# A decoder layer on one core: the work of all five engines put in another order

## The reference

```python
x = _layernorm(x + _L0_attn_ref(x, W_qkv, W_out))                 # 16 heads of 16, segments of 128, every second key
x = _layernorm(x + _L0_xattn_ref(x, ctx_1024, ctx_1024, Wq, ...)) # 77 context rows
x = _layernorm(x + _L0_ffn_ref(x, router_w, w1, b1, w2, b2))

# _L0_ffn_ref
logits = x @ router_w                         # 14 experts
assignments = jnp.argmax(logits, axis=-1)
weights = jnp.take_along_axis(jax.nn.softmax(logits, axis=-1), assignments[:, None], axis=1)[:, 0]
hid = jax.nn.gelu(jnp.einsum('nd,edf->nef', x, w1) + b1, approximate=False)
all_out = jnp.einsum('nef,efd->ned', hid, w2) + b2
moe_out = jnp.take_along_axis(all_out, assignments[:, None, None], axis=1)[:, 0, :] * weights[:, None]
```

## Time and profile before

| | |
|---|---|
| median of 3 runs | 597.56 us (596.89 to 598.15) |
| the profiled execution | 593.98 us, of it 592.2 us span |
| mean granted clock of TensorE | 0.977 of full speed |
| PE busy | 560.5 us, 95% of the span |
| DVE busy | 463.3 us, 78% |
| POOL busy | 405.7 us, 69% |
| ACT busy | 343.1 us, 58% |
| chain that ended last | PE 74%, POOL 9%, issue 7%, DVE 5% |

### The profile page before, as it was taken

One profiled execution on the slowest core, in us unless ns is written; L12 is line 12 of the kernel. 1 busy time (PEld: TensorE's weight loads), 2 busy tenths in 40 slices (PEclk: granted clock), 3 DMA queues, 4 the chain that ended last, 5 costly groups with the idle time before them and its releaser, 6 DMA issues.

```text
span 592.2 us, 16640 instructions
## 1 busy us (share of the span) xinstructions
PE 560.5 (95%) x5608; PEld 474.9 (80%) x5608; DVE 463.3 (78%) x1071; ACT 343.1 (58%) x842; POOL 405.7 (69%) x554
## 2 busy tenths in 40 slices
PE   7989999999999999999999999799799999999990
PEld 5867788788888888788788778568789999999990
DVE  3778999999999999999999989865455555666661
ACT  2456666666666676676666765546545555555540
POOL 4446675678678677678678766675787677777652
PEclk9899999999999999999999999969989999999996
DMA  7416026126225314313514101114343333333200
GB/s 216 162 24 191 14 52 196 27 68 183 42 60 160 65 40 137 103 51 88 153 34 144 52 10 37 34 39 119 53 112 97 85 87 87 95 92 89 68 16 0
DMA packets 76692, 50.11 MB, mean 85 GB/s; under 512 B 39222, under 2 KB 70970, under 8 KB 76608
## 3 DMA queue, kind: packets, MB, share of 16 engines
q1 hardware_dynamic: 71264, 40.60, 25.5%
q0 software_dynamic: 5344, 8.44, 5.5%
HBM read 40.55 MB, written 10.60 MB: 86 GB/s over the span
## 4 chain that ended last, share of the span: by engine, by line
PE 74%; POOL 9%; issue 7%; DVE 5%; ACT 2%; DMA 1%; POOLq 0%; ACTq 0%; DVEq 0%
PE ps_r L822 15%; PE ps_r L740 13%; PE ps_s L956 11%; PE ps_r L972 10%; PE ps_r L807 5%; PE ps_r L902 5%; PE ps_s L762 4%; PE ps_s L753 3%; POOL token_lists L1579 3%; POOL prob L1498 2%; PE ps_r L795 2%; PE ps_r L879 2%; PE ps_r L897 2%; PE ps_r L904 2%; POOL out L1605 1%
## 5 line engine op out<-in xcount | busy, mean ns | idle before, releaser
L1498 POOL TENSOR_TENSOR prob<-prob,rden 128x616 f32<-128x616 f32 (+1 forms) x96 | 138.4, 1449 | 56.8 <-DVE rden L1173 55.1
L999 ACT COPY probT<-ps_r 128x512 f32<-128x512 f32 x192 | 86.8, 480 | 43.2 <-PE ps_r L740 41.4
L1141 DVE TENSOR_REDUCE mx<-ps_s 128x8 f32<-128x616 f32 (+1 forms) x96 | 88.8, 925 | 19.1 <-PE ps_s L753 12.8
L1019 ACT ACTIVATE prob<-prob 128x616 f32<-128x616 f32 (+1 forms) x96 | 79.4, 833 | 33.8 <-DVE prob L1152 33.6
L1161 DVE TENSOR_REDUCE den<-prob 128x8 f32<-128x616 f32 (+1 forms) x96 | 88.3, 920 | 6.9 <-ACT prob L1019 5.7
L1152 DVE TENSOR_TENSOR prob<-ps_s,mx 128x616 f32<-128x616 f32 (+1 forms) x96 | 89.8, 936 | 4.5 <-PE ps_r L740 3.0
L956 PEld LDWEIGHTS ps_s<-xgT,w1b 128*128 128x128 f32 x720 | 88.0, 193 | 2.5 <-issue 0.3
L740 PE MATMUL ps_r<-ident,prob 128*128 128x128 f32 (+1 forms) x576 | 88.4, 281 | 1.6 <-POOL prob L1498 1.0
L956 PE MATMUL ps_s<-xgT,w1b 128*128 128x128 f32 x720 | 88.6, 276 | 0.2 <-ACT xgT L1107 0.2
L972 PE MATMUL ps_r<-w2s,hT 128*128 x360 | 86.2, 383 | 0.3 <-ACT hT L1119 0.3
L740 PEld LDWEIGHTS ps_r<-ident,prob 128*128 128x128 f32 (+1 forms) x576 | 66.1, 142 | 16.8 <-issue 9.6
(11 more groups left out here) (158 smaller groups left out, 1006.1 us busy)
## 6 DMA issues: line engine op xcount, KB each, us to landing
w1s<-in_w SPq DMA_DIRECT2D x14, 512.0 KB
w2s<-in_w SPq DMA_DIRECT2D x14, 512.0 KB
b2r<-in_b SPq DMA_DIRECT2D x45, 128.0 KB, 3.2
xT<-in_x_cols SPq DMA_DIRECT2D x16, 256.0 KB, 2.9
xres<-in_x SPq DMA_DIRECT2D x16, 256.0 KB
x_rows<-x2s SPq DMA_DIRECT2D x32, 128.0 KB, 1.9
xkT<-in_xk_cols SPq DMA_DIRECT2D x16, 128.0 KB, 2.3
ctxT<-in_ctx_cols SPq DMA_DIRECT2D x16, 77.0 KB, 2.1
```

Of the source, the lines that this page charges most:

```text
L999: nc.scalar.copy(probT[0:rows, par, first:last], src[0:rows, 0:last - first]).then_inc(pT_copied[kind].sem, 1)
L1019: nc.scalar.activation(prob[:, n % 3, 0:width], prob[:, n % 3, 0:width], ACT.Exp, scale=SCALE).then_inc(exp_done[kind].sem, 1)
L1141: nc.vector.tensor_reduce(m, s, axis=AX, op=ALU.max).then_inc(max_done[kind].sem, 1)
L1498: nc.gpsimd.tensor_tensor(p, p, rden[:, par, 0:heads, None].to_broadcast([P, heads, width]), ALU.mult).then_inc(scaled[kind].sem, 1)
```

## The change

No operation, buffer or amount of work differs: PE still has 703 steps, DVE 1,062, ACT 663, POOL 392 and SP 268. Their order is new in all five lists, and `HELD` names another set of implied waits to go with it. From the diff (a line or two of each kind):

```diff
-        PE_FIRST = """
-            q0:0 k0:0 v0:0 scores0:0 wr0:0 wr1:0 scores1:0 k0:1 q0:1 wr2:0 vx0:0 scores0:1 probT00:0 probT01:0
+            q0:0 k0:0 v0:0 scores0:0 k0:1 wr0:0 wr1:0 scores1:0 q0:1 wr2:0 vx0:0 scores0:1 probT00:0 probT01:0
...
-            gelu:1 rt1:15 rows:2 rows:3 wa:2 wa:3 gelu:2 gate_exp0:15 wa:4
+            wa:2 rows:1 gelu:0 wa:3 rt1:15 gelu:1 rows:2 rows:3 gate_exp0:15 wa:4 gelu:2
...
-        PE_TILES = "y@2 hid@0 rows@-1"
-        ACT_TILES = "wa@-2 rows@-2 gelu@-1"
-        DVE_TILES = "eps@1 bias@0 wd@-4 res@0 stat@0 norm@1 agg@0"
-        POOL_TILES = "gather@-3 pow@3 put@4"
-        SP_TILES = "slots@-2 bias_row@-2"
+        PE_TILES = "y@3 hid@1 rows@0"
+        ACT_TILES = "rows@-1 gelu@0 wa@-3"
+        DVE_TILES = "agg@4 eps@4 bias@3 wd@-2 res@3 stat@3 norm@4"
+        POOL_TILES = "pow@3 put@4 gather@-4"
+        SP_TILES = "bias_row@4 slots@-3"
```

More of the change, by code:

```diff
@@ L32 @@
 HELD = {
[L33 to L37, removed]
@@ L332, in decoder_layer @@
-            attend3:0 v0:2 ox0:0 probT40:0 x1T0:1 scores1:2 probT41:0 probT50:0 attend4:0
+            attend1:1 scores5:0 oa1:1 probT20:0 probT21:0 vx0:1 scores0:2 probT30:0 probT31:0 attend2:0
+            attend3:0 v0:2 ox0:0 scores1:2 probT40:0 x1T0:1 probT41:0 probT50:0 attend4:0 probT51:0 qx0:1
         """
         PE_ORDER = """
-            probT51@4 qx0@3 probT00@2 probT01@2 attend5@4 scores2@3 ox1@4 attend0@2 scores3@3 probT10@2
-            probT11@2 oa0@2 scores4@3 attend1@2 k0@1 oa1@2 probT20@3 scores5@3 probT21@3 q0@1 probT30@3 v0@1
@@ L337, in decoder_layer @@
-            scores0@1 probT31@3 kx0@2 vx0@2 attend2@3 attend3@3 scores1@1 probT40@3 x1T0@2 probT41@3 ox0@3
-            probT50@3 probT51@3 qx0@2 probT00@1 attend4@3 attend5@3 scores2@2 probT01@1 ox1@3 scores3@2 k0@0
-            probT10@1 attend0@1 scores4@2 probT11@1 oa0@1 rk0@5 attend1@1 scores5@2 probT20@2 oa1@1 q0@0
-            probT21@2 probT30@2 probT31@2 v0@0 scores0@0 attend2@2 attend3@2 probT40@2 probT41@2 ox0@2 attend4@2
-            scores1@0 x1T0@1 vx0@1 probT50@2
+            probT00@2 probT01@2 attend5@4 scores2@3 ox1@4 attend0@2 scores3@3 probT10@2 probT11@2 oa0@2
@@ new lines, in decoder_layer @@
+            attend1@2 scores4@3 k0@1 oa1@2 probT20@3 scores5@3 probT21@3 q0@1 probT30@3 v0@1 scores0@1 kx0@2
+            probT31@3 vx0@2 attend2@3 attend3@3 scores1@1 probT40@3 probT41@3 x1T0@2 ox0@3 probT50@3 probT51@3
+            qx0@2 probT00@1 attend4@3 scores2@2 attend5@3 probT01@1 ox1@3 scores3@2 k0@0 probT10@1 attend0@1
+            scores4@2 probT11@1 oa0@1 attend1@1 scores5@2 probT20@2 rk0@5 oa1@1 probT21@2 q0@0 probT30@2
+            probT31@2 v0@0 scores0@0 attend2@2 attend3@2 probT40@2 probT41@2 ox0@2 attend4@2 scores1@0 x1T0@1
@@ L342, in decoder_layer @@
+            vx0@1 probT50@2 probT51@2 qx0@1
         """
         PE_LAST = """
-            probT51:12 qx0:13 probT00:14 probT01:14 attend5:12 scores2:13 ox1:12 attend0:14 scores3:13
-            probT10:14 k0:15 probT11:14 scores4:13 q0:15 attend1:14 scores5:13 probT20:13 probT21:13 oa0:14
-            oa1:14 vx0:14 probT30:13 probT31:13 scores0:15 attend2:13 kx0:14 probT40:13 probT41:13 probT50:13
-            attend3:13 attend4:13 scores1:15 probT51:13 x1T0:14 ox0:13 qx0:14 v0:15 scores2:14 attend5:13 rk0:11
@@ L353, in decoder_layer @@
-            attend5:15 rows:0 rk0:13 hid:0 rows:1 ox1:15 hid:1 y:0 rows:2 rows:3 y:1 hid:2 tot0:1 rk0:15 rows:4
-            hid:3 y:2 spr0:1
+            probT00:14 probT01:14 attend5:12 scores2:13 ox1:12 attend0:14 scores3:13 probT10:14 k0:15 probT11:14
+            scores4:13 q0:15 scores5:13 attend1:14 probT20:13 probT21:13 oa0:14 oa1:14 probT30:13 scores0:15
+            attend2:13 probT31:13 vx0:14 probT40:13 attend3:13 probT41:13 probT50:13 scores1:15 attend4:13
+            kx0:14 x1T0:14 probT51:13 ox0:13 qx0:14 v0:15 scores2:14 attend5:13 probT00:15 rk0:11 scores3:14
@@ L362, in decoder_layer @@
+            qx0:1 take_o5:0 probT00:2 probT01:2
         """
         ACT_ORDER = """
[L364 to L367 removed]
```

185 lines of the change are left out of this document (94 added, 91 removed).

## The result

The changed kernel is slower: 604.13 us median (602.11 to 605.02, 6 runs) against 597.86 (596.89 to 600.26, 6 runs), a ratio of 1.0104 with the interval 1.0078 to 1.0130, +6.3 us. I had forecast 597.8 us and no measurable change.

What follows compares the result with a forecast made beforehand. TensorE, nearly always busy, was taken as the bound. Terms -0.4 + 0.2 - 0.4 + 0.5 - 0.1 = -0.2, or +0.2 with the handover at +0.9, rounded to +0.3: 597.56 + 0.3 = 597.8 us, range 594.2 to 601.5.

Steps and rivals of the forecast that it cites:

- What bounds the kernel: Whole kernel: TensorE busy 299.28 of 300 us, so only its idle time and clock can move the end.
- The period: Six repeats in the batches: later `ox0` +0.8, VectorE and ring copies -0.1 each; sum +0.2, bound +1.8 us.
- The term for `ox0`: Period: a `v0` copy ahead of `take_o3` delays `ox0` by 0 to 0.37, chosen 0.13; six times +0.8 us.
- The -0.6 for a freer ring and an earlier `less_max4`: Period: VectorE brings `less_max4` earlier and the ring's copies leave their banks sooner, -0.1 in each of six.
- Rival C: Slower through the period: six stalls of 0.3 us and more, or 38 tiles of 0.05; +1.8 to +4, 600.5 us; chance 0.10.
- The start: First batches: `k0:1` fills a wait before `scores1:0`; 1.0 us gain at most, taken as -0.4 because the clock may fall.
- 1 MB at 280 to 370 GB/s: Start: `wout` and residual loads come behind 1 MB of expert weights, 3 to 4 us later; taken as 0.
- Batches 14 and 15 and the handover: Last batches -0.4 by shorter waits; handover +0.5, where moved attends cost +0.9 unless the clock returns a window earlier.
- the row from 383.6: Handover: a window busy 3.04 of 3.40 us, still followed by clock 0.50, taken to speak against an early clock.
- `x1r` ahead of the gather: Handover: `x1r`, 1.29 us, delays the gather of tile 0; cost 0 while `rows:0` stays at 398.68 or later.
- The first tiles: `wa:2` ahead of `gelu:0` +0.6, `ln20:15` out of the way -0.4, gather of tile 7 -0.3; sum -0.1 us.
- The tiles: Order per tile changes only in phase and TensorE has no idle time: 0, with +1.9 us as the bound.

Runs made afterwards that it cites:

- pe_back: The changed kernel with TensorE's period order of the kernel before (five pairs of steps swapped back): 599.35 us, ratio 1.0075 against before.
- ctrl_waits: The order before on every engine, with 13 more groups of waits kept than in the kernel before: 598.64 us, ratio 1.0054.
- keep_tiles: The kernel before with two groups of VectorE waits kept that run only in the tiles: 597.54 us, ratio 1.0004.
- again_before: The kernel before, unchanged, run again for a second profile: 595.09 us, with before on that chip at 594.96.
- third_before: The kernel before, unchanged, run once more for a third profile: 596.78 us, with before at 597.35.
- k1_loaded: The kernel before with k of batch 1 between the first and second scores and its load ahead of the small weights: 636.67 us, ratio 1.0000.
- after_end: The order before until batches 14 and 15 are half way, then the changed order for the rest: 601.79 us, ratio 1.0111 against before.
- keep_pe: The kernel before with TensorE's five left-out groups of waits for a bank kept: 599.11 us, ratio 1.0072.

## Why the prediction was wrong

- **What bounds the kernel** failed first: "nothing there can win more than 0.7 us in all" took idle time for all the slack there is. Matmuls overlap, and a release that comes a few tenths late only stretches what is drawn busy. By the steps' start times 5.3 us lay in A over the least times, and the change added 3.6 to them.
- **The period**, predicted +0.2 with +1.8 as its bound, measured +4.7 (A). This is the step that made the forecast wrong. The term for `ox0` was 0.13 us each by choice, where the whole copy (0.37) was the upper end: it was 0.40 each, 2.4 us, at `probT41` (0.16) and `ox0` (0.24), of which the wait at `probT50` took 0.8 back. The copy had been going on while TensorE worked on the attends; behind `take_o2` it starts when they are done. I had seen the copy ahead of both `take_o` in the earlier trace rows and priced its length, not its new start. TensorE's own changed order had no term at all: `scores2` between the attends (1.7, 0.35 of it by kept waits), `kx0` ahead of `probT31` (0.3); `pe_back` gives back 2.7 in all. Nor had VectorE's late `reciprocal` of batches 13 and 14 (0.7). The -0.6 for a freer ring and an earlier `less_max4` is not to be seen in any of these stretches. Rival C had the right place and sign, for the most part the wrong engine, and 0.10.
- **The waits that the new order doesn't imply** were named nowhere. `HELD` had 82 names and has 65, and the program has 34 instructions more, though I said the work was the same: 0.6 us in A by `ctrl_waits`, and with the pause and the gather up to 3.8 us.
- **The start**, -0.4 with -1.0 at best: -0.55 from `q:0` to `q:3`, in each of three profiles. The sum of +0.1 up to batch 3 holds a first step that is 0.7 us later by chance. The size was right, the way to it in part luck. From `q:0` TensorE was 1.5 us ahead at `scores5:0`, and 0.9 of it were gone at `qx0:1`, in the list for the start, which no term held. And idle of this size (1.57 of 3.40) does not by itself lower the clock: `keep_tiles` has the same gap and 1.00 behind it. What the start wins over before is that the clock did not fall. A slip beside it: 1 MB at 280 to 370 GB/s is 2.7 to 3.6 us, not 3 to 4; nothing hung on it.
- **Batches 14 and 15 and the handover**, together +0.1 in the sum: measured -0.2 in C, inside its scatter. The attends filled the gaps and the clock came back 3.4 us earlier, which the row from 383.6 had made me hold for unlikely. What that is worth can be estimated from before alone: with 10.2 us at half clock C is 56.0 and 56.1, with 13.7 us in `again_before` 57.4. So 3.4 us less of it give about 1.3 back, and since C did not move, the attends cost about as much, within the 0 to 1.4 of the term. By the Trainium skill's page "TensorE: Matmul & The Clock Gate", section "Part 4: PE-mode transpose", the handover was to cost +0.9; the window from 393.2 has transposes, the plan and attends in it, the next one is at 1.00, and so the rule could not be told from its opposite here. `x1r` ahead of the gather held nobody up: `rows:0` starts with no wait.
- **The first tiles**, -0.1: `hid:4` came 0.8 us later, and from `rows:0` to the issue of the gather of tile 7 pass 25.8 us, as before (25.9). All of it was hidden by the wait for the gather, as said. Its landing was left at 5.8 us, one value of one execution; in three profiles it is 5.8, 6.4 and 7.5 before and 8.5, 7.4 and 8.2 after. That is D, +1.8, with a half clock of 6.8 us behind the long wait in each of the three after; `third_before` has that too.
- **The tiles**, 0: right, 137.00 of 137.

What stays open: why the core loses time near 203 us, why the clock at the start falls in some executions, and how much of D is the changed order. The pause is no matter of order, since six other programs that run the order before up to there have it. The traces show a fetch of instructions within 2 us of it, also in the kernel before, which doesn't stop, so that is no proof. The chip or its condition adds its own: in the session of `k1_loaded` there were such stops all along. Of the measured +6.3 us about 4.7 are the order of the batches and its waits, 3.9 of them given back by two edits; the start takes 0.5 off, and the rest lies in B and D.

## What to carry over

When an engine is busy for 99.8% of a stretch, count its instructions or compare the start times of the same steps: short waits hide inside overlapped work, and six repeats of 0.8 us look like no idle time at all. Price a moved step by when it can start at its new place, with its load and with the waits that the old order made needless, not by its length. Look at three profiles before trusting a gap of a microsecond: the landing of one gather scattered by more than most terms of this sum, and so did the first step. Count from a step and not from the start of the span, and what looked like 0.1 or 0.2 us becomes 0.55 and 1.0, the same in each profile.

## What was not expected of the hardware

- Near 203 us the core loses 0.4 to 3.7 us in all 14 profiles other than those of the unchanged kernel (that of `k1_loaded` left out), and nothing in three profiles of that. In six of the 14 there is a time, 0.3 to 1.5 us, in which no engine works at all; in the others some engine always works, and TensorE waits for up to 1.8 us. In `after_end`, `keep_pe` and `keep_tiles` TensorE's clock fell to half behind it.
- The same start, with the same gap of 1.6 us on TensorE, was followed by half clock in six profiles and by full clock in three. It is worth 1.3 us.
- 14 satisfied waits on SyncE came with +0.31% (0.07 to 0.55) in 12 runs, and with no time in A.
- In one session the kernel before took 639.67 us, in the others 595 to 598 us. The profile of that session has stops of all engines at several places and a mean granted clock of 0.948.
- Between one attend and the next TensorE takes at least 0.46 us from start to start, between an attend and scores or transposes at least 0.55. The same steps repeat to 0.01 us in three profiles, so even 0.05 us of a single repeat can be read.
